# A selective scan laid out as 4 states by 32 channels, with TensorE forming its input term

## The chip, the cores and the metric

The program runs on one NeuronCore of one Trainium2 chip. The metric is the device time of one launch in microseconds; lower is better.

## The reference

The program is two transformer-like layers. The change touches the Mamba block of the second layer. With `x` of 2 sequences by 2048 positions by 256, it computes:

```
xz = layernorm(x) @ w_in            # 512 channels of x_path, 512 of z_path
x_path = silu(conv4(x_path) + b_conv)
B, C = x_path @ w_b, x_path @ w_c   # 16 states each
delta = softplus(x_path @ w_delta + b_delta)
A = -exp(A_log)                     # 512 channels by 16 states
for t:                              # per channel d and state n
    h = exp(delta[t] * A) * h + (delta[t] * x_path[t]) * B[t]
    y[t] = sum over n of h * C[t]  +  D * x_path[t]
out = (y * silu(z_path)) @ w_out
```

Everything is fp32. There are 512 channels, 16 states, and 4096 positions in all (two sequences of 2048, each with its own state).

## The kernel before

The stages run one after the other, each in its own block with an allocator whose prefix names its tiles: attention (`ag`, `qkv`, `att`, `ao`), a mixture of experts (`ex`, `mo`), then `scan_inputs` (tiles `si_...`), `selective_scan` (tiles `ss_...`), and an fp4 feed-forward (`wt`, `fp`). A block ends when all five engines have ended their part of it. Inside a block each engine has its own written-out list of instructions, and semaphores join the lists; nothing reorders them.

**scan_inputs** works on 8 groups of 512 positions (`GROUPS`, `GN`), all 512 channels at once as four tiles of 128 (`DT`). `run_stages` writes one engine's steps for all groups, each step shifted by so many groups. TensorE (PE) forms `xz` from `si_xn_t` (L2014), `delta` before its softplus (L2025), and B and C (L2030). VectorE (DVE) convolves, and makes `xc` (the silu of the convolution, L1903), `zs` and `delta` (L1914). ScalarE (ACT) does the exponentials and logarithms and copies PSUM to SBUF. GpSimd (POOL) multiplies `dx = delta * xc` (L1827). Then `delta` and `dx` are each split into three bf16 parts whose sum is the fp32 value: DVE casts the high part (L1840, L1845), POOL subtracts (L1815, L1817), ACT makes the middle part (L1955). SyncE (SP) stores the six parts, 512 KB each, to `scratch.steps`, and `xc`, `zs`, B and C beside them.

**selective_scan** takes 256 units. A unit is 1024 positions (`HALF`, half a sequence) of 8 channels by 16 states on the 128 partitions; 16 units with the same 128 channels and positions make a part. Per unit: SP loads the six bf16 rows of its 8 channels (`ss_stack`, 96 KB); PE spreads them over the partitions with bf16 tables of ones (`spread_x` into `ss_ps_x`, L2304; `spread_d` into `ss_ps_d`, L2314, which has two slots and so waits for an older scan); ACT makes the decay in place in `ss_ps_d` (L2240); `u` is `ss_ps_x` times B. For two units of three DVE makes `u` (L2254); for the third (`n % 3 == 2`) ACT copies `ss_ps_x` (L2237) and POOL multiplies (L2204). DVE runs the scan (L2266), one instruction over 1024 positions; the second half of a sequence starts from the last column of `h`. POOL multiplies `h` by C (`ss_ch`, L2215). PE sums over states into `ss_ps_y` (`sums`, L2336): four fp32 matmuls of 32 output columns of the array each and 256 positions per unit, five units behind the last of their group of four. Once a part, PE adds D times x (`skip_term`, L2325) and DVE multiplies by `zs` (`gate`, L2274).

## Time and profile before

| | us |
|---|---|
| median of 3 runs | 4137.14 |
| lowest and highest of them | 4123.6, 4149.17 |
| the profiled execution | 4119.56 |
| its span | 4117.7 |
| mean granted TensorE clock in it, as a share of full speed | 0.858 |

All rows below are of the profiled execution. The span is the time from the first to the last instruction; the profiled execution is 1.9 us longer than its span, and 17.6 us shorter than the median. In the span, `scan_inputs` lies at 2388 to 2797, `selective_scan` at 2797 to 3627, the feed-forward behind that. TensorE has two clock levels, 1.2 and 2.4 GHz, which read 0.50 and 1.00 as granted clock.

### The profile page before, as it was taken

What the parts mean: (1) busy time and instruction counts of PE and PEld (TensorE: products, weight loads), DVE (VectorE), ACT (ScalarE), POOL (GpSimd) and SP (SyncE); (2) the same over time, 40 slices, a digit from 0 to 9 for tenths busy, and PEclk for the clock granted to TensorE, in tenths of its full rate; (3) what the DMA queues carried; (4) which work ended last, traced back from release to release, by engine and by line L of the source; (5) the groups of instructions that cost most, each with busy time, mean ns of one, the idle gap of its engine ahead of it and who ended that gap; (6) DMA issues with size and microseconds to landing.
All of it is one profiled execution on the core that took longest, in us unless ns stands there. A gap on an engine that the chain in (4) does not pass through costs nothing. (4 is left out here: it accounts for less than half of the span.)

```text
span 4117.7 us, 50542 instructions
## 1 busy us (share of the span) xinstructions
PE 3344.1 (81%) x16354; PEld 1530.2 (37%) x16355; DVE 3214.5 (78%) x4733; ACT 2031.6 (49%) x2575; POOL 1531.3 (37%) x1012
## 2 busy tenths in 40 slices
PE   5769999999999999695997678646778877847876
PEld 2433333333333333274665433211111111125665
DVE  5659999999999999244442559987999999957996
ACT  0317777777777777531111656643444444415453
POOL 0100000000000000023003605567999999946775
PEclk8869999999999999867999789876776677769998
DMA  1662203031230300332222533332122212121110
GB/s 51 237 158 28 45 4 46 4 45 18 32 45 4 46 4 4 104 123 87 65 65 80 169 107 114 129 124 84 63 70 75 72 63 64 62 72 54 51 41 18
DMA packets 221697, 280.48 MB, mean 68 GB/s; under 512 B 40313, under 2 KB 163458, under 8 KB 218786
## 3 DMA queue, kind: packets, MB, share of 16 engines
q1 hardware_dynamic: 204658, 244.47, 21.8%
q0 software_dynamic: 6144, 17.05, 1.3%
q10 hardware_dynamic: 10688, 16.32, 1.1%
q8 instruction: 116, 1.90, 0.2%
q14 instruction: 91, 0.75, 0.1%
HBM read 152.56 MB, written 124.57 MB: 67 GB/s over the span
## 5 line engine op out<-in xcount | busy, mean ns | idle before, releaser
L909 DVE TENSOR_REDUCE att_maxima<-att_ps_m 128x1 f32<-128x512 f32 x2048 | 1275.4, 682 | 163.4 <-PE att_ps_m L965 158.7
L864 ACT ACTIVATE att_probs<-att_ps_s 128x1024 f32<-128x1024 f32 x1024 | 998.4, 1021 | 383.0 <-PE att_ps_s L980 379.1
L965 PE MATMUL att_ps_m<-att_ks,att_qs 48*128 48x512 f32 x2048 | 743.3, 487 | 71.9 <-DMA att_ks<-scratch_k 28.6
L2215 POOL TENSOR_TENSOR ss_ch<-ss_h,ss_c_rep 128x1024 f32<-128x1024 f32 x256 | 594.1, 2345 | 0.7 <-DVE ss_h L2266 0.6
L965 PEld LDWEIGHTS att_ps_m<-att_ks,att_qs 48*128 48x128 f32 x2048 | 300.0, 188 | 757.7 <-DVE att_maxima L909 650.2
L991 PE MATMUL att_ps_o<-att_probs,att_vs 128*32 128x512 f32 x4096 | 546.4, 605 | 0.5 <-ACT att_probs L864 0.5
L2240 ACT ACTIVATE ss_ps_d<-ss_ps_d,ss_a_neg 128x1024 f32<-128x1024 f32 x256 | 278.6, 1088 | 417.4 <-PE ss_ps_d L2314 417.4
L980 PE MATMUL att_ps_s<-att_qs,att_ks 50*128 50x512 f32 x2048 | 466.1, 401 | 1.8 <-ACT att_probs L864 0.7
L2266 DVE TENSOR_TENSOR_SCAN ss_h<-ss_ps_d,ss_h,ss_u 128x1024 f32<-128x1024 f32 x128 | 296.0, 2334 | 5.5 <-ACT ss_ps_d L2240 2.4
L2314 PE MATMUL ss_ps_d<-ss_stack,ss_spread 96*128 96x512 bf16 x512 | 213.7, 511 | 97.5 <-DVE ss_h L2266 91.9
L2266 DVE TENSOR_TENSOR_SCAN ss_h<-ss_ps_d,ss_u 128x1024 f32<-128x1024 f32 x128 | 288.2, 2274 | 5.9 <-issue 3.1
L980 PEld LDWEIGHTS att_ps_s<-att_qs,att_ks 50*128 50x128 f32 x2048 | 279.2, 186 | 34.1 <-ACT att_probs L864 23.7
L837 POOL TENSOR_TENSOR att_m_parts<-att_m_t,att_m_parts 16x128 fp32r<-16x128 f32 x32 | 14.3, 448 | 737.4 <-ACT att_m_parts L884 737.4
L844 POOL TENSOR_TENSOR att_heads<-att_o_t,att_sums 128x256 f32<-128x256 f32 x32 | 19.9, 621 | 705.2 <-DVE att_sums L924 705.2
L2304 PE MATMUL ss_ps_x<-ss_stack,ss_spread 96*128 96x512 bf16 x512 | 217.7, 519 | 66.8 <-DVE ss_u L2254 61.7
L2336 PE MATMUL ss_ps_y<-ss_ch,ss_sum_block 128*32 128x256 f32 x2048 | 217.8, 511 | 4.0 <-POOL ss_ch L2215 4.0
L2254 DVE TENSOR_TENSOR ss_u<-ss_ps_x,ss_b_rep 128x1024 f32<-128x1024 f32 x171 | 204.7, 1197 | 16.4 <-PE ss_ps_x L2304 16.4
L2204 POOL TENSOR_TENSOR ss_u<-ss_x_copy,ss_b_rep 128x1024 f32<-128x1024 f32 x85 | 199.4, 2345 | 25.7 <-ACT ss_x_copy L2237 25.7
L2014 PE MATMUL si_ps_xz<-si_xn_t,si_w_in 128*128 128x512 f32 x256 | 128.8, 662 | 74.0 <-ACT si_xp L1983 57.4
L1639 POOL DMA_INDIRECT mo_back<-scratch_sorted_y,moe_packed x64 | 61.7, 964 | 339.2 <-DMA mo_b_norm<-in_b_norm 318.4
L1435 ACT ACTIVATE ex_y<-ex_ps_y,ex_x 128x256 f32<-128x256 f32 x72 | 34.2, 475 | 303.1 <-PE ex_ps_y L1506 303.1
L1488 PE MATMUL ex_ps_h<-moe_w_w,ex_x_t 128*128 x288 | 137.4, 600 | 0.4 <-issue 0.4
(404 smaller groups left out, 5026.5 us busy)
## 6 DMA issues: line engine op xcount, KB each, us to landing
...
ss_stack<-scratch_steps SPq DMA_DIRECT2D x256, 96.0 KB
...
```

What stands on the lines that cost most here:

```text
L864: act.activation(probs[:, (2 * n + pair) % 4, :, :], ps_s[pair][:, :, :], ACT.Exp, scale=HD ** -0.5).then_inc(exp_done, 1)
L909: dve.tensor_reduce(maxima[:, j, at:at + 1], ps_m[plan.bank(key)][:, :], AX.X, ALU.max).then_inc(maxed, 1)
L965: pe.matmul(ps_m[plan.bank(key)][:, :], qs[own, s // QC % 2, s % QC, p, t * P:(t + 1) * P], ks[own, s // QC % 2, p, c * GN:(c + 1) * GN], ...
L980: mm = pe.matmul(ps_s[pair][:, e, :], ks[rows_of(e, 0, ROWS), st // QC % 2, pair, kt * P:(kt + 1) * P], qs[rows_of(e, 0, ROWS), st // QC % ...
L991: mm = pe.matmul(ps_o[h * VW:(h + 1) * VW, :], vs[st // QC % 2][:, kt, h * VW:(h + 1) * VW], probs[:, (2 * n + h // 2) % 4, h % 2, :], sta ...
L2215: pool.tensor_tensor(ch[:, w.n % (CH_GROUPS * JQ), :], h[:, w.i, :], c_rep[:, w.half, :], ALU.mult).then_inc(s["ch_ready"], 1)
L2240: act.activation(ps_d[:, w.n % 2, :], ps_d[:, w.n % 2, :], ACT.Exp, scale=a_neg[:, at:at + 1]).then_inc(s["decay_ready"], 1)
L2254: dve.tensor_tensor(u[:, w.n % U_SLOTS, :], ps_x[:, :], b_rep[:, w.half, :], ALU.mult).then_inc(s["u_ready"], 1)
L2266: dve.tensor_tensor_scan(h[:, w.i, :], ps_d[:, w.n % 2, :], u[:, w.n % U_SLOTS, :], start, ALU.mult, ALU.add).then_inc(s["h_ready"], 1)
L2304: mm = pe.matmul(ps_x[:, q * GN:(q + 1) * GN], spread[:, 1, :], stack[:, w.n % STACKS, q * GN:(q + 1) * GN], start=True, stop=True)
L2314: mm = pe.matmul(ps_d[:, w.n % 2, q * GN:(q + 1) * GN], spread[:, 0, :], stack[:, w.n % STACKS, q * GN:(q + 1) * GN], start=True, stop=True)
L2336: mm = pe.matmul(ps_y[jq * 32:(jq + 1) * 32, cols], block[:, jj, :], ch[:, (part * JJ + jj) % CH_GROUPS * JQ + jq, cols], start=False, sto ...
```

## The change

**The scan's layout.** A unit is still 1024 positions and 128 rows of (channel, state), 256 units, 16 to a part, but now 4 states (`NSUB`) by 32 channels (`DSUB`). The order of parts becomes four chunks of 1024 positions, with the four channel tiles inside each; a chunk that is the second of its sequence starts from `ss_carry`, a column that ACT copies out of `h` (`keep_state`). `h` has 4 slots (`H_SLOTS`) where it had 16.

**u.** PE forms `u` by itself (`make_u`): for each 64 positions, `dx` turned (64 positions by 32 channels) is the stationary operand and a diagonal matrix with B of one state on its diagonal (64 by 64, `ss_diag`) the moving one. That is 8 blocks x 2 halves of the array's rows x 4 column groups (the states) = 64 fp32 matmuls a unit, each of 64 rows, 32 output columns and 64 positions, into one of three pairs of PSUM banks (`ss_ps_u`). ACT builds the 512 diagonals in 64 calls of `build_diag`, eight small ACTIVATEs each, from the turned B (`ss_b_t`): 32 ACTIVATEs ahead of the first unit, eight beside each of the next 12 units, and eight beside each of 16 units around every one of the three changes of chunk. The multiplications by B on DVE and POOL, the copies for them and the replicated B are gone.

**The decay.** SP loads fp32 `delta` of 32 channels four times over (`ss_delta`, 512 KB, four per part, six slots), and ACT writes `exp(delta * A)` to SBUF (`ss_decay`, three slots). The scan reads the decay from SBUF and `u` from PSUM, where it read them the other way about. POOL has only `ss_ch` left. The sums and the skip term keep their shapes.

**scan_inputs.** The six bf16 parts, their casts, subtractions and middle copies go. `delta` is stored as fp32 (1 MB a group). DVE makes `dx`; PE turns it (16 transposes of 128 by 128 a group, and 4 small ones for B and C) into the banks that `xz` uses; ACT copies it to SBUF in four copies of 512 columns and one of 128; SP stores it (1 MB). POOL has nothing left but memsets. SP also lays `A_log` out in the scan's order, in 16 transfers of 512 single fp32 elements each.

The diff, cut:

```diff
...
+                with nc.allow_non_contiguous_dma("the scan's order of states and channels"):
+                    by = io["A_log"].rearrange("(l g s) (q h) -> s h (l g) q", l=8, g=4, s=4, h=4)
+                    for state in range(4):
+                        for eight in range(4):
+                            at = (state * 4 + eight) * 8
+                            sp.dma_start(scratch.a_rows[at:at + 8, :].rearrange("l (g q) -> (l g) q", g=4), by[state, eight]).then_inc(s["a_laid"], 16)
...
-                    sp.wait_ge(s["low_ready"], g * 2 + i + 1)
-                    for part in reversed(range(i * PARTS, (i + 1) * PARTS)):
-                        sp.dma_start(tiles(scratch.steps[part, :, :], g), parts[:, part, :, :]).then_inc(s[stored], 16)
...
+                    sp.wait_ge(s["delta_ready"], g + 1)
+                    sp.dma_start(tiles(scratch.delta, g), val[:, slot, 0, :, :]).then_inc(s["delta_stored"], 16)
+                def store_turned(g, slot):
+                    sp.wait_ge(s["dx_copied"], (g + 1) * GT)
+                    sp.dma_start(rows_at(scratch.dx_t, g * GN), dx_t[:, :, :]).then_inc(s["dx_stored"], 16)
+                    sp.wait_ge(s["b_copied"], g + 1)
+                    sp.dma_start(rows_at(scratch.b_t, g * GN), b_t[:, :, :]).then_inc(s["b_stored"], 16)
...
-                def split(i, g, slot):
...
-                    pool.tensor_tensor(v, v, parts[:, i * PARTS, :, :], ALU.subtract).then_inc(s["rest_ready"], 1)
...
-                    pool.tensor_tensor(parts[:, i * PARTS + 2, :, :], v, parts[:, i * PARTS + 1, :, :], ALU.subtract).then_inc(s["low_ready"], 1)
...
-                    pool.wait_ge(s["delta_ready"], g + 1)
-                    pool.tensor_tensor(val[:, slot, 1, :, :], val[:, slot, 0, :, :], xc[:, slot, :, :], ALU.mult).then_inc(s["dx_ready"], 1)
...
-                    dve.tensor_copy(parts[:, 0, :, :], val[:, slot, 0, :, :]).then_inc(s["high_ready"], 1)
...
+                def delta_x(g, slot):
...
+                    dve.tensor_tensor(val[:, slot, 1, :, :], val[:, slot, 0, :, :], xc[:, slot, :, :], ALU.mult).then_inc(s["dx_ready"], 1)
...
-                    act.wait_ge(s["rest_ready"], g * 2 + i + 1)
-                    act.activation(parts[:, i * PARTS + 1, :, :], val[:, slot, i, :, :], ACT.Copy).then_inc(s["mid_ready"], 1)
...
+                def copy_turned(g, slot):
+                    for t in range(GT):
+                        act.wait_ge(s["dx_turned"], g * GT + t + 1)
...
+                        act.activation(dx_t[:, t, :], ps_xz[t % XZ][:, :], ACT.Copy).then_inc(s["dx_copied"], 1)
...
+                    act.activation(b_t[:, :, :].rearrange("p t n -> p (t n)"), ps_xz[GT % XZ][:, 0:GT * 2 * NS], ACT.Copy).then_inc(s["b_copied"], 1)
...
+                def turn(g, slot):
+                    pe.wait_ge(s["dx_ready"], g + 1)
+                    for t in range(GT):
...
+                            pe.wait_ge(s["xz_copied"], (min(g + 3, GROUPS) if isinstance(g, int) else g + 3) * 2 * DT)
...
+                        for o in range(DT):
+                            mm = pe.transpose(ps_xz[t % XZ][:, o * P:(o + 1) * P], val[:, slot, 1, o, t * P:(t + 1) * P], ident[:, :])
+                        mm.then_inc(s["dx_turned"], 1)
+                    for t in range(GT):
+                        mm = pe.transpose(ps_xz[GT % XZ][:, t * 2 * NS:(t + 1) * 2 * NS], bc[:, t * P:(t + 1) * P], ident[0:2 * NS, 0:2 * NS])
+                    mm.then_inc(s["bc_turned"], 1)
...
-                run_stages(pe, GROUPS, (product_xc, 1), (product_xz, -1))
...
+                run_stages(pe, GROUPS, (product_xc, 1), (turn, 2), (product_xz, -1))
...
-STACKS, U_SLOTS = 4, 3
...
+DELTAS, DECAYS, U_BANKS, H_SLOTS = 6, 3, 3, 4
...
-        self.on_pool = n % 3 == 2
-        self.pool = (n + 1) // 3
...
+        self.ng, self.dq = self.i // DQ, self.i % DQ
...
-                    sp.dma_start(stack[0:PARTROWS, w.n % STACKS, :], scratch.steps[:, row:row + DG, w.cols]).then_inc(stack_loaded[w.n % STACKS], 16)
...
+                    sp.dma_start(delta[:, k % DELTAS, :], over(scratch.delta[first:first + DSUB, cols:cols + HALF].unsqueeze(0), [NSUB, DSUB, HALF])
...
+                def load_dx(part):
...
+                    at = part // DT * HALF
+                    for half in range(2):
+                        rows = scratch.dx_t[at + half * (HALF // 2):at + (half + 1) * (HALF // 2), part % DT * P:(part % DT + 1) * P]
+                        sp.dma_start(dx_t[half * RT:(half + 1) * RT, part % 2, :, :], rows.rearrange("(j p) d -> p j d", p=RT)).then_inc(dx_loaded[part % 2], 16)
...
+                    sp.dma_start(c_rep[:, ng, :], over(rows.unsqueeze(1), [NSUB, DSUB, HALF])).then_inc(c_loaded[ng], 16)
...
-                    pool.tensor_tensor(u[:, w.n % U_SLOTS, :], x_copy[:, w.pool % 2, :], b_rep[:, w.half, :], ALU.mult).then_inc(s["pool_u_ready"], 1)
...
+                        pool.wait_ge(s["y_steps"], w.n // DQ - CH_GROUPS + 1)
+                    pool.tensor_tensor(ch[:, w.n % (CH_GROUPS * DQ), :], h[:, w.n % H_SLOTS, :], c_rep[:, w.ng, :], ALU.mult).then_inc(s["ch_ready"], 1)
             @blk.scalar
...
+                for half in range(2):
+                    rows = scratch.b_t[:, 0:NS].rearrange("(c h j p) n -> h p c j n", c=CHUNKS, h=2, p=RT)[half]
+                    for chunk in range(CHUNKS):
+                        act.dma_start(b_t[half * RT:(half + 1) * RT, chunk, :, :], rows[:, chunk, :, :]).then_inc(s["b_loaded"], 16)
...
+                def build_diag(chunk, ng, q):
+                    if chunk > 0 and q == 0:
+                        act.wait_ge(s["u_ready"], (chunk * DT - 1) * GROUPS_HERE + (ng + 1) * DQ)
+                    for m in range(q * PIECE, (q + 1) * PIECE):
+                        j, n = m // NSUB, ng * NSUB + m % NSUB
+                        ins = act.activation(diag[:, j, n, :], ident_two[:, :], ACT.Copy, scale=b_t[:, chunk, j, n:n + 1])
+                    ins.then_inc(s["diag_ready"], 1)
+                def make_decay(w):
...
+                    act.activation(decay[:, w.n % DECAYS, :], delta[:, w.delta % DELTAS, :], ACT.Exp, scale=a_neg[:, at:at + 1]).then_inc(s["decay_ready"], 1)
...
+                    act.activation(carry[:, w.state:w.state + 1], h[:, w.n % H_SLOTS, HALF - 1:HALF], ACT.Copy).then_inc(s["carried"], 1)
...
+                    make_decay(w)
+                    if w.n >= DECAYS and not units[w.n - DECAYS].second:
+                        keep_state(units[w.n - DECAYS])
+                    if w.n < (NG - 1) * DQ:
+                        build_diag(0, w.ng + 1, w.dq)
...
+                    if w.dt == DT - 1 and w.ng > 0 and w.chunk + 1 < CHUNKS:
+                        build_diag(w.chunk + 1, w.ng - 1, w.dq)
+                    if w.dt == 0 and w.ng == 0 and w.chunk > 0:
+                        build_diag(w.chunk, NG - 1, w.dq)
...
-                    dve.tensor_tensor_scan(h[:, w.i, :], ps_d[:, w.n % 2, :], u[:, w.n % U_SLOTS, :], start,
+                    dve.wait_ge(s["u_ready"], w.n + 1)
...
+                    if w.second:
+                        dve.wait_ge(s["carried"], w.carried)
+                        start = carry[:, w.state:w.state + 1]
+                    dve.tensor_tensor_scan(h[:, w.n % H_SLOTS, :], decay[:, w.n % DECAYS, :], ps_u[w.n % U_BANKS][:, :], start,
...
+                    if w.part > 0 and w.i == SUMS_TO - 1:
+                        gate(w.part - 1)
+                    scan(w)
+                gate(PARTS_HERE - 1)
...
+                def make_u(w):
+                    if w.i == 0:
+                        pe.wait_ge(dx_loaded[w.part % 2], (w.part // 2 + 1) * 2 * 16)
+                    if w.dt == 0 and w.dq == 0:
+                        pe.wait_ge(s["diag_ready"], diag_built(w.chunk, w.ng))
+                    if w.n >= U_BANKS:
+                        pe.wait_ge(s["h_ready"], w.n - U_BANKS + 1)
+                    for j in range(BLOCKS):
+                        for half in range(2):
+                            own, at = slice(half * RT, (half + 1) * RT), half * (HALF // 2) + j * RT
+                            for q in range(NSUB):
+                                mm = pe.matmul(ps_u[w.n % U_BANKS][q * DSUB:(q + 1) * DSUB, at:at + RT], dx_t[own, w.part % 2, j, w.dq * DSUB:(w.dq + 1) * DSUB],
+                                               diag[own, j, w.ng * NSUB + q, :], start=True, stop=True)
+                    mm.then_inc(s["u_ready"], 1)
...
-                        mm = pe.matmul(ps_x[:, q * GN:(q + 1) * GN], spread[:, 1, :], stack[:, w.n % STACKS, q * GN:(q + 1) * GN],
...
-                        mm = pe.matmul(ps_d[:, w.n % 2, q * GN:(q + 1) * GN], spread[:, 0, :], stack[:, w.n % STACKS, q * GN:(q + 1) * GN],
...
+                        mm = pe.matmul(ps_y[dq * DSUB:(dq + 1) * DSUB, cols], block[:, :], ch[:, (part * NG + ng) % CH_GROUPS * DQ + dq, cols],
...
                 for w in units:
-                    spread_x(w)
                     if w.i == SUMS_FROM:
-                        skip_term(w)
+                        skip_term(w.part)
                     sums_at(w.n)
-                    spread_d(w)
...
```

PE in the scan, around the skip term of a part, before (`ss_ps_x` and `ss_ps_d` are the spread dx and delta, `ss_ps_y` the output sums):

```order
L2304 MATMUL ss_ps_x<-ss_stack,ss_spread 128x512 x2
L2325 MATMUL ss_ps_y<-ss_xc,ss_skip 128x512 x2
L2336 MATMUL ss_ps_y<-ss_ch,ss_sum_block 32x256 x4
L2314 MATMUL ss_ps_d<-ss_stack,ss_spread 128x512 x2
L2304 MATMUL ss_ps_x<-ss_stack,ss_spread 128x512 x2
L2336 MATMUL ss_ps_y<-ss_ch,ss_sum_block 32x256 x4
```

With the change PE has there (`ss_ps_u` is the input term u, three slots):

```order
L2305 MATMUL ss_ps_u0<-ss_diag,ss_dx_t 32x64 x64
L2317 MATMUL ss_ps_y<-ss_xc,ss_skip 128x512 x2
L2326 MATMUL ss_ps_y<-ss_ch,ss_sum_block 32x256 x4
L2305 MATMUL ss_ps_u1<-ss_diag,ss_dx_t 32x64 x64
L2326 MATMUL ss_ps_y<-ss_ch,ss_sum_block 32x256 x4
L2305 MATMUL ss_ps_u2<-ss_diag,ss_dx_t 32x64 x64
```

The two spreads of two matmuls each become one group of 64; sums and skip term stand ahead of it as they stood ahead of `spread_d`.

ACT at the head of the scan, before:

```order
L2222 ACTIVATE ss_a_neg<-ss_a_neg 128x64
L2224 ACTIVATE ss_skip<-all_ident,ss_d_col 128x128 x4
L2226 ACTIVATE ss_a_neg<-ss_a_neg 128x64
L2229 ACTIVATE ss_b_rep<-ss_ps_d 128x1024
L2231 ACTIVATE ss_c_rep<-ss_ps_d 128x1024
L2240 ACTIVATE ss_ps_d<-ss_ps_d,ss_a_neg 128x1024 x2
L2237 ACTIVATE ss_x_copy<-ss_ps_x 128x1024
```

With the change ACT has there:

```order
L2198 DMA ss_a_neg<-scratch_a_rows 128x64
L2202 DMA ss_b_t<-scratch_b_t 64x8x16 x8
L2203 DMA ss_d_col<-in_D_param 128x4
L2206 ACTIVATE ss_ident_two<-all_ident 64x64 x2
L2209 ACTIVATE ss_sum_block<-all_ident 32x32 x4
L2211 ACTIVATE ss_a_neg<-ss_a_neg 128x64
L2213 ACTIVATE ss_a_neg<-ss_a_neg 128x64
L2221 ACTIVATE ss_diag<-ss_ident_two,ss_b_t 128x64 x32
L2229 ACTIVATE ss_decay<-ss_delta,ss_a_neg 128x1024
L2221 ACTIVATE ss_diag<-ss_ident_two,ss_b_t 128x64 x8
```

The loads of the turned B and 32 diagonals stand ahead of the first decay; the skip tables moved behind the first units.

SP at the head of `scan_inputs`, before:

```order
L1764 DMA si_w_in<-in_w_in 128x2x1024
L1765 DMA si_w_conv<-in_w_conv 128x16
L1767 DMA si_b_conv<-in_b_conv 128x4
L1767 DMA si_b_delta<-in_b_delta 128x4
L1780 DMA si_xn_t<-scratch_xn_t 128x2x512 x3
```

With the change SP has there:

```order
L1765 DMA si_w_in<-in_w_in 128x2x1024
L1766 DMA si_w_conv<-in_w_conv 128x16
L1768 DMA si_b_conv<-in_b_conv 128x4
L1768 DMA si_b_delta<-in_b_delta 128x4
L1775 DMA scratch_a_rows<-in_A_log 512x1x1 x16
L1785 DMA si_xn_t<-scratch_xn_t 128x2x512 x3
```

The 16 transfers of `A_log` stand between the small loads and the first loads of the normalised input.

## Rows read from the trace of the kernel before

**Rows 1.** Windows of the scan: window, length, PE, PEld, DVE, ACT, POOL, PEclk, DMA share, GB/s
```profile
2900.00:3000.00 100.00, 79.67 (x394) 18.64 (x392) 97.69 (x56) 45.07 (x42) 99.21 (x44) 0.72 0.20 63
3001.40:3002.60 1.20, 1.19 (x9) 0.20 (x8) 1.20 (x1) 1.16 (x2) 1.20 (x1) 0.50 0.11 22
3007.00:3007.80 0.80, 0.70 (x9) 0.16 (x8) 0.80 (x1) 0.72 (x1) 0.80 (x2) 1.00 0.00 0
```

**Rows 2.** Groups of the scan, 2820 to 3600: busy us, mean ns, idle
```profile
L2215 POOL TENSOR_TENSOR ss_ch<-ss_h,ss_c_rep 128x1024 f32<-128x1024 f32 x249 | 577.9, 2345 | 0.7 <-DVE ss_h L2266 0.6
...
L2254 DVE TENSOR_TENSOR ss_u<-ss_ps_x,ss_b_rep 128x1024 f32<-128x1024 f32 x166 | 198.7, 1197 | 7.5 <-PE ss_ps_x L2304 7.5
```

**Rows 3.** Lines by source: ns min/median/max, first and last start us
```profile
L2266 DVE TENSOR_TENSOR_SCAN ss_h<-ss_ps_d,ss_u x128: 2251/2276/2292, 2813.4 to 3563.6; 128x1024 f32<-128x1024 f32 x128
L2266 DVE TENSOR_TENSOR_SCAN ss_h<-ss_ps_d,ss_h,ss_u x128: 2311/2336/2351, 2861.6 to 3612.3; 128x1024 f32<-128x1024 f32 x128
...
L2274 DVE TENSOR_TENSOR ss_gated<-ss_ps_y,ss_zs x16: 1189/1216/1225, 2881.9 to 3622.5; 128x1024 f32<-128x1024 f32 x16
```

**Rows 4.** Waits, 2820 to 3600: us in total, times, longest
```profile
ACT ss_ps_d L2240 <- PE ss_ps_d L2314: 407.7, 244, 6.2
...
DVE ss_u L2254 <- PE ss_ps_x L2304: 7.5, 6, 1.7
```

**Rows 5.** Timeline of the scan: start us, us, engine, line, records
```profile
3000.34 4.58 DVE L2266 TENSOR_TENSOR_SCAN ss_h<-ss_ps_d,ss_h,ss_u 128x1024 f32<-128x1024 f32 x2
...
3001.51 1.08 PE L2336 MATMUL ss_ps_y<-ss_ch,ss_sum_block 128*32 128x256 f32 x8
...
3005.30 6.96 POOL L2215 TENSOR_TENSOR ss_ch<-ss_h,ss_c_rep 128x1024 f32<-128x1024 f32 x3
...
3007.06 0.64 PE L2336 MATMUL ss_ps_y<-ss_ch,ss_sum_block 128*32 128x256 f32 x8
...
3610.62 4.13 PE L2336 MATMUL ss_ps_y<-ss_ch,ss_sum_block 128*32 128x256 f32 x40
```

**Rows 6.** Timeline of TensorE in the attention and router stages
```profile
804.42 0.40 PE L980 MATMUL att_ps_s<-att_qs,att_ks 50*128 50x512 f32 x2
...
1857.84 0.24 PE L1368 MATMUL ao_ps_c<-ao_both,ao_all_ones 128*128 128x8 bf16 x4
1857.94 1.07 PE L1335 MATMUL ao_ps_x<-all_ident,moe_rows 128*128 128x128 f32 x8
```

**Rows 7.** Page, part 3: the queue that fetches instructions
```profile
q8 instruction: 116, 1.90, 0.2%
```

**Rows 8.** Line by source: one load of 4096 four-byte pieces
```profile
L815 SPq DMA_DIRECT2D scratch_b_rows<-in_b x1: 14220/14220/14220, 306.8 to 306.8; - x1
```

**Rows 9.** Timeline of the scan's head
```profile
2797.59 0.36 SPq L2109 DMA_DIRECT2D ss_a_neg<-in_A_log  x1
...
2799.86 1.26 ACT L2224 ACTIVATE ss_skip<-all_ident,ss_d_col 128x128 f32<-128x128 f32 x4
...
2805.37 1.02 ACT L2229 ACTIVATE ss_b_rep<-ss_ps_d 128x1024 f32<-128x1024 f32 x1 [4.11 <-PE ss_ps_d L2292]
```

**Rows 10.** Window of scan_inputs, its steady part (columns as in 1)
```profile
2423.20:2721.40 298.20, 228.14 (x492) 92.33 (x492) 284.84 (x198) 182.92 (x179) 144.65 (x30) 0.88 0.34 116
```

**Rows 11.** Line by source: the product that makes xc
```profile
L1903 DVE TENSOR_TENSOR si_xc<-si_conv,si_sig_c x8: 2291/6154/6158, 2423.2 to 2721.4; 128x2048 f32<-128x2048 f32 x8
```

**Rows 12.** Groups of scan_inputs, 2423.2 to 2721.4
```profile
L2014 PE MATMUL si_ps_xz<-si_xn_t,si_w_in 128*128 128x512 f32 x212 | 107.6, 666 | 57.4 <-ACT si_xp L1983 57.4
...
L1840 DVE CAST si_parts<-si_val 128x2048 bf16<-128x2048 f32 x6 | 24.7, 4114 | 0.6
```

**Rows 13.** Timeline of scan_inputs' end
```profile
2720.12 5.32 POOL L1817 TENSOR_TENSOR si_parts<-si_val,si_parts 128x2048 bf16<-128x2048 f32 x1 [2.02 <-ACT si_parts L1955]
...
2764.62 5.53 POOL L1827 TENSOR_TENSOR si_val<-si_val,si_xc 128x2048 f32<-128x2048 f32 x1 [4.56 <-DVE si_val L1914]
...
2786.26 4.05 POOL L1817 TENSOR_TENSOR si_parts<-si_val,si_parts 128x2048 bf16<-128x2048 f32 x1 [2.02 <-ACT si_parts L1955]
```

436 lines of the change are left out of this document (180 added, 256 removed).

## The prediction

> **What bounds the kernel now.** I read the windows first, then the groups and the waits of the scan, then the timeline of single units. In the scan two engines are full at once: in a window of 100 us DVE is busy 97.7 and POOL 99.2, against 80 for PE and 45 for ACT [rows 1]. The waits say the same from the other side: ACT waits 408 us of 780 for PE's spread, while DVE's largest wait on another engine for its own u is 7.5 us [rows 4]. Per unit DVE does a scan of 2.28 or 2.34 us and, for two units of three, a product of 1.20 us; POOL does `ss_ch` at 2.35 us and, for one of three, the same again for u [rows 2, 3]: DVE 2.31 + 0.80 = 3.11, POOL 2.35 x 1.33 = 3.13. The loop runs from the first scan at 2813.4 to the end of the last gate at 3622.5 + 1.2 = 3623.7 [rows 3], 810.3 us or 3.165 a unit. So what DVE and POOL lose, the loop gains, until something else is late. In `scan_inputs` DVE is full too, 284.8 us of 298.2 [rows 10], but not by its own work: the product that makes `xc` takes 2.29 us at best and 6.15 in the median [rows 11], and the last one starts 1.3 us into a subtraction of POOL [rows 11, 13]. Two DVE operations with SBUF operands are stretched by POOL's splits, a cast to 4.1 us among them [rows 12].
>
> **The scan's loop, engine by engine.** DVE keeps scans and gates: two scans in a row take 4.58, so 2.29 each [rows 5]; 256 x 2.29 + 16 x 1.22 = 606 us. POOL keeps `ss_ch`: three in 6.96 [rows 5], 256 x 2.32 = 594. The scan still reads one operand from SBUF and one from PSUM, so I take its price as unchanged. Both engines now end within 2% of each other, and PE and ACT must stay under 2.3 us a unit.
>
> PE: a step of the sums is four fp32 matmuls in four column groups and shows as 8 records, so one such matmul is two passes. The eight take 1.08 us at granted clock 0.50 and 0.64 at 1.00 [rows 1, 5], and a stream of 40 takes 4.13 [rows 5]: ten rounds of four, 0.41 us each at the lower clock for 256 columns. The column groups do run side by side. Two records on the two halves of the array's rows take 0.40 together, as long as one [rows 6], so row halves run side by side as well; both together, eight tiles, no row shows. If they do, `make_u` is 64 x 2 / 8 = 16 rounds of 64 columns: a quarter of 0.41, 0.10 to 0.11 us a round at the lower clock, 1.7 us; at the upper clock a quarter of 0.32 (0.64 / 2), 0.08, so 1.3 us. With the sums (1.08 or 0.64) and 0.2 for the two changes of shape, an estimate, PE needs 3.0 us a unit at the lower clock and 2.1 at the upper. At the mix of before, 0.72 [rows 1], that is 0.56 x 3.0 + 0.44 x 2.1 = 2.6, above the 2.29 of DVE. But PE has three slots of u to run ahead in, and when it is the late one it has no idle time. I take 0.1 us a unit, +26, between 0 and 256 x 0.31 = +79.
>
> ACT: the decay is one pass over 128 x 1024, like the 1.02 us copy [rows 9], and the carried column is small (0.2, an estimate). A diagonal is 128 x 64; four of 128 x 128 took 1.26, 0.315 each [rows 9]. A 64-column one lies between half of that and all of it; I take 0.25. Eight beside a unit are 2.0 us, so ACT needs 3.2 in those units, 0.9 too much. They are 12 + 3 x 16 = 60 units: 54, less what the two decays made ahead cover at each chunk change (3 x 5), 39, and a part of that lies in units where PE is late anyway. I take +30, between 0 (0.16 each) and +90 (0.315 each).
>
> At a part's boundary the gate waits for the last sums, and the skip term, queued ahead of sums and `make_u` on PE, waits for the gate. DVE has two scans, 4.6 us, until it needs that u; skip term, sums and `make_u` need 3 to 4.5. Cost 0 to 20 us over 15 boundaries; I take 10. The loop: 606 + 26 + 30 + 10 = 672, against 810: **-138**.
>
> **The scan's head.** Before, the first scan comes 2813.4 - 2797.6 = 15.8 us after the start [rows 3, 9]. With the change ACT first issues eight loads of 512 pieces of 64 bytes. A transfer of 4096 four-byte pieces occupied its queue for 14.22 us [rows 8], 3.5 ns a piece; I take the same per piece, so 14.2 us for these 4096. Then 2 us of landing, 32 diagonals at 0.25 (8 us) and a first u and decay of 3: 27 to 28. **+12**, between -2 and +18. Nothing hides this: every engine waits for the first u.
>
> **scan_inputs.** Head: the 16 transfers of `A_log` are 8192 four-byte pieces on SP, ahead of the first load of the input, so 8192 x 3.47 ns = 28.4 us in which PE has no input. **+28**, between +6 (if a transfer cost what a small load costs, 0.36 [rows 9]) and +33. Middle: `xc` is made eight times from 2423.2 to 2721.4 [rows 11], 42.6 us apart. Without splits and casts DVE's own work is some 30 us a group, and ACT's about 27. PE is next: 228.1 / 7 = 32.6 [rows 10], 16 + 4 transposes of which eight take 1.07 [rows 6], 2.7, and its waits for ACT's copies, 57.4 / 7 = 8.2 before [rows 12], of which I keep 4.5, as ACT must empty the same banks of the turned dx too. So 39.8 a group, **-18** for seven, between -46 and 0. Tail: delta of the last group is there at 2764.6, the last split ends at 2790.3, and the scan starts 7.3 later [rows 9, 13]. Now delta comes some 6 us sooner (its chain on DVE is no longer stretched), then dx 2.3, turning 2.7, a last copy 0.7, and the same 7.3: 2771.6. **-26**, between -15 and -32. These terms sum to -4 without the scan's loop, with +12 of its head in it.
>
> **Sum.** -138 + 12 + 28 - 18 - 26 = -142 on the profiled execution of 4119.6, so 3978. The median of the runs is 17.6 above that execution; on it the forecast is 4137 - 142 = **3995**.
>
> **The rivals.** First, PE stays at its lower clock. Then it needs 3.0 to 3.1 us a unit and sets the pace: 256 x 3.05 = 781, -29, and with the -4 some **4104**, from 4090 to 4125: no change to speak of. For it: the clock is 0.72 at 80% busy PE [rows 1]. Against: at 3 us a unit PE would be busy all the time, which it is not now.
>
> Second, and on the slower side: **what one matmul costs however short it is**. 64 matmuls of two passes are 128 pairs of weight load and matmul in each unit, with 64 columns each. The densest row of the trace has four bf16 matmuls of 8 columns in 0.24 us, where one takes 0.17 [rows 6]: 23 ns apart, though each has only 8 columns. If such a gap holds between tiles too, `make_u` costs 128 x 23 ns = 2.9 us, with sums and changes 3.8 a unit: 256 x 3.8 + 20 = 993, +183 - 4, **4316**. It decides from 3.1 us a unit on, that is from 17.6 ns a pair. If only the row halves fail to overlap, `make_u` is 32 rounds of 80 to 107 ns, 2.6 to 3.4 us, and the unit 3.4 to 4.7: 4210 and up. The instruction stream works the same way: its queue fetched 116 packets, 1.90 MB [rows 7], one in 35 us, and the change gives PE some 230 more instructions in every unit. Against it: eight records of four tiles fit in 0.64 us, which leaves little room for a gap between tiles, but four tiles of 256 columns would hide one. This is the rule of the Trainium skill that speaks against the change: "TensorE: Matmul & The Clock Gate", section "Wait — 56ns, not 53.3ns?", says that start-to-start never drops below about 25 ns however few the columns. Read as a limit on every pair it would make `make_u` 3.2 us and the time some 4380. The same section gives 62 ns a matmul when decoding is done in software, which would be 7.9 us a unit; the 23 ns of [rows 6] rule that out here.
>
> Third, small ones: diagonals, piece-wise loads and boundaries all at their dear ends, +60 + 6 + 5 + 10 on the forecast, 4076.
>
> **Chances.** The forecast with its own range 3935 to 4080 (PE's cover, ACT's builds, the head's and the input stage's bounds): 0.56. PE at its lower clock: 0.17, of which 0.04 below 4096. The pair cost, row halves or fetch: 0.24, from 4180 to 4400. Something outside these, better or worse: 0.03. The range must reach into the second rival: 3935 to 4290 leaves out about 0.03 below and 0.14 above. One per cent, 41 us, is about what a measurement of this kernel can tell from no change: faster 0.61, same 0.14, slower 0.25.
>
> **What the profile of the changed kernel would show.** Right: scans 2.3 us apart over most of the loop, POOL with next to no idle time, the `make_u` group at 1.3 to 1.7 us from first to last record with eight tiles starting within a few tens of ns, granted clock above 0.75 in the scan, and pauses of DVE only around the chunk changes, ended by ACT's decay. If instead DVE waits mostly for `ss_ps_u`, the granted clock tells the first rival (near 0.5) from the second (near 1.0, pairs 20 ns or more apart). In `scan_inputs` the first `si_xn_t` load should be issued some 28 us later than before, `xc` should come every 40 us at 2.3 us each, and the scan should start about 16 us sooner than before. The prediction fails most likely at the step that lets eight tiles of 64 columns run at the rate of four of 256.

## The result and the profile after

The kernel with the change takes 4412.95 us (median of 4, 4404.66 to 4428.87), against 4141.94 for the kernel before in the same comparison: a ratio of 1.069, 95% interval 1.066 to 1.072. It is slower by 271 us. The forecast was 3995 in a range up to 4290. The profiled execution took 4428.87, its span is 4427.1, 309.4 longer than that of before.

The page, with the head of the span, part 1 (busy us, share, instructions) and the queue that fetches instructions, which answers to [rows 7]:

```profile
span 4427.1 us, 114206 instructions
PE 3409.8 (77%) x48250; PEld 1855.4 (42%) x48251; DVE 2922.0 (66%) x4552; ACT 2080.2 (47%) x3158; POOL 1149.9 (26%) x864
...
q8 instruction: 364, 5.96, 0.6%
```

PE has 48,250 matmul records where it had 16,354, and the instruction queue fetched 364 packets of 16 KB where it had fetched 116. Yet PE's busy time rose by 66 us only, from 3344.1. Windows of 100 us in the scan (columns as in [rows 1], which they answer to):

```profile
3000.00:3100.00 100.00, 67.08 (x3110) 42.75 (x3091) 53.24 (x25) 50.61 (x142) 54.24 (x23) 0.75 0.23 73
3500.00:3600.00 100.00, 62.13 (x3157) 41.33 (x3150) 53.63 (x24) 28.71 (x47) 54.48 (x24) 0.83 0.27 76
```

Nothing is full any more: DVE and POOL fell from 98 and 99 to some 54, PE is at 62 to 67. The granted clock is 0.75 and 0.83 in these two windows, higher than the 0.72 of before. Scans and gates by source (as [rows 3]) and the waits of 2830 to 3900 (as [rows 4]):

```profile
L2273 DVE TENSOR_TENSOR_SCAN ss_h<-ss_decay,ss_ps_u x128: 2260/2287/2290, 2838.0 to 3658.4; 128x1024 f32<-128x1024 f32 x128
L2273 DVE TENSOR_TENSOR_SCAN ss_h<-ss_decay,ss_carry,ss_ps_u x128: 2320/2347/2349, 3106.7 to 3924.8; 128x1024 f32<-128x1024 f32 x128
...
L2281 DVE TENSOR_TENSOR ss_gated<-ss_ps_y,ss_zs x16: 1224/1225/1226, 2929.2 to 3931.7; 128x1024 f32<-128x1024 f32 x16
```

```profile
POOL ss_ch L2194 <- DVE ss_h L2273: 920.3, 235, 444.7
ACT ss_decay L2229 <- DVE ss_h L2273: 594.9, 196, 7.1
...
DVE ss_h L2273 <- PE ss_ps_u L2305: 434.8, 184, 64.8
...
DVE ss_h L2273 <- ACT ss_decay L2229: 27.6, 19, 3.6
```

The durations are those of before. The loop is 3931.7 + 1.2 - 2838.0 = 1094.9 us, 4.28 a unit, where it was 810.3. DVE waits 435 us for `ss_ps_u`, 65 of them before the first scan; the wait for ACT's decay, for which the forecast had a term of 30, is 28. The timeline shows what PE does in that time:

```profile
3300.57 2.35 DVE L2273 TENSOR_TENSOR_SCAN ss_h<-ss_decay,ss_carry,ss_ps_u 128x1024 f32<-128x1024 f32 x1 [1.19 <-PE ss_ps_u L2305]
...
3300.98 0.81 PE L2305 MATMUL ss_ps_u<-ss_diag,ss_dx_t 64*32 64x64 f32 x58
3303.00 2.36 POOL L2194 TENSOR_TENSOR ss_ch<-ss_h,ss_c_rep 128x1024 f32<-128x1024 f32 x1 [1.16 <-DVE ss_h L2273]
...
3303.12 0.93 PE L2305 MATMUL ss_ps_u<-ss_diag,ss_dx_t 64*32 64x64 f32 x70 [1.33 <-issue]
...
3303.97 0.64 PE L2326 MATMUL ss_ps_y<-ss_ch,ss_sum_block 128*32 128x256 f32 x8
...
3304.13 2.35 DVE L2273 TENSOR_TENSOR_SCAN ss_h<-ss_decay,ss_carry,ss_ps_u 128x1024 f32<-128x1024 f32 x1 [1.22 <-PE ss_ps_u L2305]
...
3304.54 0.74 PE L2305 MATMUL ss_ps_u<-ss_diag,ss_dx_t 64*32 64x64 f32 x50
...
3307.26 1.02 PE L2305 MATMUL ss_ps_u<-ss_diag,ss_dx_t 64*32 64x64 f32 x78 [1.98 <-issue]
...
3308.38 2.35 DVE L2273 TENSOR_TENSOR_SCAN ss_h<-ss_decay,ss_carry,ss_ps_u 128x1024 f32<-128x1024 f32 x1 [1.90 <-PE ss_ps_u L2305]
```

In the second row 58 matmul records (an fp32 matmul makes two), each with its weight load, run in 0.81 us, the last of them alone some 0.2: a new pair of load and matmul every 11 ns, so the eight tiles do overlap, as the forecast had it. Then PE does nothing for 1.33 us, in the middle of a `make_u`, and its idle time is put down to "issue": no semaphore is waited for. The next piece has 70 records of `make_u`, 8 of the sums, 50 more, then nothing until 3307.26. From one such stop to the next are 128 pairs of two instructions, 256 instructions, and 256 is what a packet of the instruction queue holds: e1 below has 256 units x 128 = 32,768 PE instructions fewer and 128 packets fewer.

In the trace's records of that queue the loop has 272 packets, as many as 256 units of 272 instructions need, a median of 3.78 us apart and never under 3.25. PE stops for more than 0.8 us 214 times in the loop, 368 us together, with 128 matmul records between two stops in the median. A packet takes 1.1 us; it starts 1.0 us before PE falls silent, and PE starts again 1.4 us after it has ended (medians; eight of ten of these restarts lie between 1.25 and 1.55 us). So what PE waits for is its next packet of instructions.

Where the 309 us went, stage by stage, from the first and last starts of the same operations in both profiles:

| | before | after | difference | forecast |
|---|---|---|---|---|
| up to the start of `scan_inputs` | 2388.2 | 2393.6 | +5.4 | 0 |
| from there to the first xc | 35.0 | 86.9 | +51.9 | +28 |
| seven intervals of xc | 298.2 | 258.2 | -40.0 | -18 |
| last xc to the scan's block | 76.2 | 44.9 | -31.3 | -26 |
| the scan's head | 15.8 | 54.4 | +38.6 | +12 |
| its loop | 810.3 | 1094.9 | +284.6 | -138 |
| the rest | 494.0 | 494.2 | +0.2 | 0 |

The product that makes xc, by source, answers to [rows 11]; it is at its 2.29 us every time, now that POOL is silent. Behind it stands the window of the seven intervals (columns as in [rows 1], answers to [rows 10]):

```profile
L1881 DVE TENSOR_TENSOR si_xc<-si_conv,si_sig_c x8: 2291/2293/2293, 2480.5 to 2738.7; 128x2048 f32<-128x2048 f32 x8
```

```profile
2480.50:2738.70 258.20, 233.08 (x612) 100.77 (x612) 187.92 (x193) 173.41 (x197) 0.00 (x0) 0.98 0.33 119
```

Both heads in the timeline: SP lays out `A_log`, then issues the input's load, and PE's first matmul; ACT's eight loads of the turned B, SP's four of C, the diagonals and the first scan:

```profile
2395.64 37.28 SPq L1775 DMA_DIRECT2D scratch_a_rows<-in_A_log  x16
2433.17 4.88 SPq L1785 DMA_DIRECT2D si_xn_t<-scratch_xn_t  x2
...
2456.49 15.37 PE L2022 MATMUL si_ps_xz<-si_xn_t,si_w_in 128*128 128x512 f32 x32 [68.21 <-DMA si_xn_t<-scratch_xn_t]
...
2783.98 24.87 ACTq L2202 DMA_DIRECT2D ss_b_t<-scratch_b_t  x8
...
2791.53 20.14 SPq L2141 DMA_DIRECT2D ss_c_rep<-scratch_bc  x4
...
2827.95 7.74 ACT L2221 ACTIVATE ss_diag<-ss_ident_two,ss_b_t 128x64 f32<-128x64 f32 x32 [11.91 <-DMA ss_b_t<-scratch_b_t]
...
2837.98 2.29 DVE L2273 TENSOR_TENSOR_SCAN ss_h<-ss_decay,ss_ps_u 128x1024 f32<-128x1024 f32 x1 [64.80 <-PE ss_ps_u L2305]
```

The 16 transfers occupy SP for 37.3 us, 2.3 each, and the load issued behind them lands 23 us later, where it took 7 before. ACT is busy until 2808.9 issuing its eight loads, 24.9 us; the last of them lands 19 us later, at 2827.9, and for the last 12 of these ACT does nothing but wait.

### The profile page after: what moved, and what is told of

Read it like the earlier page. It is cut to its first block and busy times, and to the rows that moved or that the text cites. A ratio compares the mean times of both kernels' runs of the same rounds, so it can differ in the third digit from the quotient of the medians.

```text
span 4427.1 us, 114206 instructions
## 1 busy us (share of the span) xinstructions
PE 3409.8 (77%) x48250; PEld 1855.4 (42%) x48251; DVE 2922.0 (66%) x4552; ACT 2080.2 (47%) x3158; POOL 1149.9 (26%) x864
## 5 line engine op out<-in xcount | busy, mean ns | idle before, releaser
L2194 POOL TENSOR_TENSOR ss_ch<-ss_h,ss_c_rep 128x1024 f32<-128x1024 f32 x256 | 604.5, 2363 | 929.4 <-DVE ss_h L2273 929.3
L2305 PE MATMUL ss_ps_u<-ss_diag,ss_dx_t 64*32 64x64 f32 x32768 | 493.9, 253 | 424.0 <-issue 364.7
L2305 PEld LDWEIGHTS ss_ps_u<-ss_diag,ss_dx_t 64*32 64x32 f32 x32768 | 402.3, 119 | 602.3 <-issue 598.4
L2229 ACT ACTIVATE ss_decay<-ss_delta,ss_a_neg 128x1024 f32<-128x1024 f32 x256 | 293.5, 1147 | 606.5 <-DVE ss_h L2273 605.8
L2273 DVE TENSOR_TENSOR_SCAN ss_h<-ss_decay,ss_ps_u 128x1024 f32<-128x1024 f32 x128 | 292.1, 2285 | 296.8 <-PE ss_ps_u L2305 253.2
L2273 DVE TENSOR_TENSOR_SCAN ss_h<-ss_decay,ss_carry,ss_ps_u 128x1024 f32<-128x1024 f32 x128 | 299.7, 2345 | 211.2 <-PE ss_ps_u L2305 189.5
L2326 PE MATMUL ss_ps_y<-ss_ch,ss_sum_block 128*32 128x256 f32 x2048 | 205.6, 464 | 25.5 <-issue 24.7
L2022 PE MATMUL si_ps_xz<-si_xn_t,si_w_in 128*128 128x512 f32 x256 | 118.2, 617 | 87.7 <-DMA si_xn_t<-scratch_xn_t 68.2
L2221 ACT ACTIVATE ss_diag<-ss_ident_two,ss_b_t 128x64 f32<-128x64 f32 x512 | 128.3, 335 | 69.6 <-PE ss_ps_u L2305 57.7
L1508 PE MATMUL ex_ps_y<-moe_w_w,ex_hid_t 128*128 x576 | 136.1, 379 | 0.0
```

What stands on the lines that cost most here:

```text
L1508: mm = pe.matmul(ps_y[slot][:, 0, :], hid_t[:, slot, f, :], w2[:, bass.ds(e, 1), f, :].rearrange("p a c -> p (a c)"), start=f == 0, stop=f ...
L2194: pool.tensor_tensor(ch[:, w.n % (CH_GROUPS * DQ), :], h[:, w.n % H_SLOTS, :], c_rep[:, w.ng, :], ALU.mult).then_inc(s["ch_ready"], 1)
L2229: act.activation(decay[:, w.n % DECAYS, :], delta[:, w.delta % DELTAS, :], ACT.Exp, scale=a_neg[:, at:at + 1]).then_inc(s["decay_ready"], 1)
L2273: dve.tensor_tensor_scan(h[:, w.n % H_SLOTS, :], decay[:, w.n % DECAYS, :], ps_u[w.n % U_BANKS][:, :], start, ALU.mult, ALU.add).then_inc( ...
L2305: mm = pe.matmul(ps_u[w.n % U_BANKS][q * DSUB:(q + 1) * DSUB, at:at + RT], dx_t[own, w.part % 2, j, w.dq * DSUB:(w.dq + 1) * DSUB], diag[o ...
L2326: mm = pe.matmul(ps_y[dq * DSUB:(dq + 1) * DSUB, cols], block[:, :], ch[:, (part * NG + ng) % CH_GROUPS * DQ + dq, cols], start=False, sto ...
```

## The experiments

The first four ask what holds PE: the array's work (the column theory), or the number of its instructions, which have to be fetched (the fetch theory, later called supply theory).

**e1_wide.** Half the instructions, the same columns.

```diff
-                    for j in range(BLOCKS):
+                    for j in range(0, BLOCKS, 2):
...
-                                mm = pe.matmul(ps_u[...][..., at:at + RT], dx_t[...], diag[own, j, w.ng * NSUB + q, :], ...)
+                                two = w.ng * NSUB + q // 2 * 2
+                                mm = pe.matmul(ps_u[...][..., at:at + 2 * RT], dx_t[...], diag[own, j, two:two + 2, :], ...)
```

> The kernel with the change, but make_u issues 32 matmuls of 128 columns a unit where it issued 64 of 64: the same columns, half the instructions. The moving operand is two neighbouring diagonals, so half of u is formed with the wrong one. Fetch theory (PE's instructions arrive in blocks of 16 KB, 364 for the whole program, and PE stands still for 1.5 to 2 us at each new one): PE instructions in a unit fall from 272 to 144, blocks in the scan from about 250 to about 135, the loop from 1095 us to 650 to 780, the time to 3970 to 4110, and the instruction queue shows some 120 packets fewer. Column theory (the array is slow on eight tiles): the columns are the same, so the time stays within 1% of 4413.

Measured: 3990.90 us, ratio 0.966 (0.964 to 0.969); loop 651.7. The page's row of the instruction queue, and a window of the scan:

```profile
q8 instruction: 236, 3.87, 0.4%
```

```profile
3200.00:3300.00 100.00, 82.08 (x2986) 47.37 (x2969) 93.79 (x45) 59.84 (x123) 97.32 (x42) 0.98 0.38 118
```

128 packets fewer, and DVE and POOL are full again, at 94 and 97. The same columns on the array fit in the time. The column theory falls.

**e2_short.** Half the columns, the same instructions. DVE also zeroes the banks of u once, before the first unit.

```diff
-                                mm = pe.matmul(ps_u[...][..., at:at + RT], dx_t[...], diag[own, j, w.ng * NSUB + q, :], ...)
+                                mm = pe.matmul(ps_u[...][..., at:at + RT // 2], dx_t[...], diag[own, j, w.ng * NSUB + q, 0:RT // 2], ...)
```

> The kernel with the change, but the 64 matmuls of make_u have 32 columns where they had 64: half the columns, the same instructions. Half of u is left at zero. Fetch theory: blocks and their stops stay, the time stays within 1% of 4413. Column theory: make_u takes half, some 0.6 us less a unit or more, the time 4413 - 150 = 4260 or lower.

Measured: 4436.31 us, ratio 1.073 (1.070 to 1.075), 0.5% above the change; loop 1104.6. Halving the columns gained nothing, with the same 364 packets:

```profile
q8 instruction: 364, 5.96, 0.6%
```

```profile
3300.00:3400.00 100.00, 65.21 (x3047) 39.78 (x3043) 54.82 (x24) 56.32 (x154) 54.26 (x24) 0.53 0.27 76
```

The granted clock is 0.53 here, where the change had 0.75 and 0.83, and the loop is the same to 1%. By itself this leaves a doubt, since half the columns at a lower clock can be as much time on the array; the trace removes it. Packets are 3.78 us apart in both. Where 128 records lie between two stops, the run takes 2.62 us here and the stop behind it 1.23, in the change 2.16 and 1.60 (medians): a longer run has a shorter stop, and run and stop are 3.75 us together in both. PE starts again 1.4 us after a packet's end in both, too. The pace is the packets', not the array's.

**e3_bf16.** Half the instructions and a quarter of the array's time.

```diff
-        diag = r.sb("diag", [P, BLOCKS, NS, RT])
-        dx_t = r.sb("dx_t", [P, 2, BLOCKS, P])
+        diag = r.sb("diag", [P, BLOCKS, NS, RT], BF16)
+        dx_t = r.sb("dx_t", [P, 2, BLOCKS, P], BF16)
```

> The kernel with the change, with the turned dx and the diagonals in bf16, which leaves out the lower part of both: one pass a matmul where fp32 takes two, so half the instructions and a quarter of the array's time in make_u. Fetch theory: 144 PE instructions a unit and nothing else on PE: loop 610 to 720, time 3930 to 4050. If DVE and POOL then set the pace, scans come 2.3 us apart over long stretches, as the forecast had it. If something outside PE (ACT's diagonals, loads) is what holds the scan, the time stays above 4250.

Measured: 3988.24 us, ratio 0.964 (0.962 to 0.967); loop 651.6. Its timeline:

```profile
3201.20 15.35 DVE L2273 TENSOR_TENSOR_SCAN ss_h<-ss_decay,ss_ps_u 128x1024 f32<-128x1024 f32 x7 [1.05 <-PE ss_ps_u L2305]
...
3203.57 13.95 POOL L2194 TENSOR_TENSOR ss_ch<-ss_h,ss_c_rep 128x1024 f32<-128x1024 f32 x6 [0.91 <-DVE ss_h L2273]
...
3205.74 0.57 PEld L2305 LDWEIGHTS ss_ps_u<-ss_diag,ss_dx_t 64*32 64x32 bf16 x64 [0.41 <-DVE ss_h L2273]
...
3206.35 0.16 PEld L2326 LDWEIGHTS ss_ps_y<-ss_ch,ss_sum_block 128*32 128x32 f32 x8
...
3208.96 0.49 PE L2305 MATMUL ss_ps_u<-ss_diag,ss_dx_t 64*32 64x64 bf16 x42 [1.77 <-issue]
```

Seven scans in 15.35 us, six products of POOL in 13.95: 2.2 and 2.3 us apart, as the forecast wanted them. PE still stops (the last row, 1.77 us of "issue"), but it has run ahead by then and nobody waits. Over the whole loop DVE's larger wait is for ACT's decay: 94.3 us ahead of all scans, 63.0 of them before the first one, so 31 inside the loop (34 in e1). The row of the scans that start from zero, the first one's 63.0 among its 86.1:

```profile
L2273 DVE TENSOR_TENSOR_SCAN ss_h<-ss_decay,ss_ps_u 128x1024 f32<-128x1024 f32 x128 | 283.4, 2270 | 94.4 <-ACT ss_decay L2229 86.1 <-issue 4.3 <-PE ss_ps_u L2305 4.0
```

**e9_bf16_96.** A dose between: e3 with 96 matmuls a unit.

```diff
-                    for j in range(BLOCKS):
+                    for j in (*range(BLOCKS // 2), *range(BLOCKS)):
```

> The bf16 version with the first four of its eight blocks formed twice: 96 matmuls a unit where it had 64, 208 PE instructions a unit where it had 144 and the change has 272, and on the array still less work than the change. Supply theory (PE gets no more than one block of 256 instructions in about 3.8 us, 14.8 ns an instruction): 208 x 14.8 ns = 3.1 us a unit, loop some 800 to 860, the time 4130 to 4200. Rival (a version in bf16 is fast because its array work is small): 0.3 to 0.5 us more array work in a unit that has room for it, the time stays within 1% of 3988.

Measured: 4161.31 us, ratio 1.011 (1.008 to 1.013); loop 835.3. Its packets and the stop in its timeline:

```profile
q8 instruction: 300, 4.92, 0.5%
```

```profile
3301.00 0.54 PEld L2305 LDWEIGHTS ss_ps_u<-ss_diag,ss_dx_t 64*32 64x32 bf16 x55 [0.41 <-issue]
...
3303.55 0.56 PE L2305 MATMUL ss_ps_u<-ss_diag,ss_dx_t 64*32 64x64 bf16 x42 [1.89 <-issue]
```

The array has less to do than in the change, and the kernel is 1.1% slower than the one before. The loop has 208 packets, 3.81 us apart (median), as in the change, though pairs start only 7 ns apart here. The supply theory named 800 to 860 for this loop from 14.8 ns an instruction, and it came out at 835. The three doses, with PE instructions a unit: 144 (e1, e3) 652 us, 208 (e9) 835, 272 (change, e2) 1095 and 1105.

**e5_more104 and e4_more52.** Instructions added to the kernel before.

```diff
+                    for m in range(104):        # e4: 52
+                        own = slice(m % 4 * 32, (m % 4 + 1) * 32)
+                        pe.matmul(ps_x[own, m * 8:(m + 1) * 8], spread[:, 1, own], stack[:, w.n % STACKS, m * 8:(m + 1) * 8], start=True, stop=True)
                     for q in range(HALF // GN):
                         mm = pe.matmul(ps_x[:, q * GN:(q + 1) * GN], spread[:, 1, :], ...)
```

> The kernel before, with 104 more matmuls of 8 columns on rotating column groups ahead of each spread_x, which write the values that spread_x then writes again: 208 more PE instructions a unit, hardly any columns. Fetch theory: some 0.85 of a block more per unit, each with a stop of 1.5 to 2 us; before has 0.15 us of slack a unit on DVE and some 0.6 on PE, so the loop grows from 810 by 150 to 400 us and the instruction queue shows some 210 packets more. Rival (eight tiles of fp32 are slow in themselves, instructions are free but for their issue): 104 pairs at 7 to 11 ns are 0.7 to 1.1 us a unit, mostly in PE's idle time, so the time grows by less than 130 us and there are no stops of over 1 us.

Measured: 4408.68 us, ratio 1.066 (1.064 to 1.068), with 208 packets more. The number lies where the fetch theory put it, but the trace gives another cause. PE's timeline and a window:

```profile
3299.82 1.03 PE L2307 MATMUL ss_ps_x<-ss_stack,ss_spread 96*128 96x512 bf16 x2
3300.79 1.08 PE L2339 MATMUL ss_ps_y<-ss_ch,ss_sum_block 128*32 128x256 f32 x8
3301.80 1.03 PE L2317 MATMUL ss_ps_d<-ss_stack,ss_spread 96*128 96x512 bf16 x2
3302.77 0.99 PE L2305 MATMUL ss_ps_x<-ss_stack,ss_spread 96*32 96x8 bf16 x104
```

```profile
3300.00:3400.00 100.00, 94.18 (x2686) 34.56 (x2684) 72.29 (x41) 33.23 (x31) 70.95 (x32) 0.55 0.24 77
```

PE is busy 94% at a granted clock of 0.55 and hardly stops: 1.0 + 1.1 + 1.0 + 1.0 us a unit, in the order of the rows, are its own work at the lower clock, 4.1 of the 4.25 us that a unit takes. The 232 instructions of a unit would come in 3.4 us at 14.8 ns each, so the supply is seldom what ends last: stops of over 0.8 us are 35, 66 us together, against 214 and 368 us in the change (those that there are end 1.5 us after a packet, as elsewhere). So e5 is no test of the supply; most of its cost is PE's own time at the lower clock. The half dose asks whether this reading holds.

> The kernel before, with 52 more matmuls of 8 columns a unit ahead of spread_x, half of the earlier dose of 104. That dose cost 276 us, with PE 94 to 96% busy at a granted clock of 0.53 and few stops: PE's own time at the lower clock, not the supply. By that reading 52 cost PE 0.5 us a unit, 4.2 - 0.5 = 3.7 us a unit at the lower clock, +100 to +150 us. By the supply theory alone 128 instructions a unit are 1.9 us and cost nothing, within 1% of before.

Measured: 4217.63 us, ratio 1.024 (1.020 to 1.028), +100 us, with PE 93 and 96% busy at a clock of 0.62 and 0.59 (the same windows as e5's, 3000 to 3100 and 3300 to 3400). That fits PE's own time, at the low end of its forecast, and not "nothing". How much of e4 and e5 is the added instructions and how much the clock, 0.72 before, was not separated.

**e8_bf16_arows and e7_bf16_heads.** The two heads, on top of e3.

```diff
 # e8: in scan_inputs
-                            sp.dma_start(scratch.a_rows[at:at + 8, :]..., by[state, eight]).then_inc(s["a_laid"], 16)
+                            pool.dma_start(scratch.a_rows[at:at + 8, :]..., by[state, eight]).then_inc(s["a_laid"], 16)
 # e7: and in selective_scan
-                    for chunk in range(CHUNKS):
-                        act.dma_start(b_t[..., chunk, :, :], rows[:, chunk, :, :]).then_inc(s["b_loaded"], 16)
+                    act.dma_start(b_t[..., 0, :, :], rows[:, 0, :, :]).then_inc(s["b_loaded"], 16)
...
-                for k in range(DQ):
-                    load_delta(k)
-                for ng in range(NG):
+                load_delta(0)
+                load_c(0, 0)
+                for k in range(1, DQ):
+                    load_delta(k)
+                for ng in range(1, NG):
                     load_c(0, ng)
...
```

> The bf16 version with the 16 transfers of A_log issued by POOL instead of SP. If they cost what the trace of the change shows (the first load of the input is issued 37 us later and lands 23 us after that, against 7 before), the first xc comes 40 to 50 us sooner and the time is 3940 to 3950. If POOL's queue still delays the input's load through the shared DMA engines, only the 37 us or less come back, and if POOL's issue runs into the end of the stage, nothing does.

Measured: 3958.54 us, ratio 0.962 (0.959 to 0.965), above the 3940 to 3950 that were expected. Against e3's ratio of 0.964 that is some 8 us, within both intervals. From the stage's start to the first xc it is 69.9 us, against 89.6 in e3: 20 us came back in the trace, half of what was expected. The timeline shows where the rest stayed:

```profile
2381.80 10.36 POOL L1818 DMA_DIRECT2D scratch_a_rows<-in_A_log  x16
2382.03 59.48 SPq L1779 DMA_DIRECT2D si_xn_t<-scratch_xn_t  x3
...
2425.03 16.08 PE L2023 MATMUL si_ps_xz<-si_xn_t,si_w_in 128*128 128x512 f32 x32 [50.55 <-DMA si_xn_t<-scratch_xn_t]
```

POOL is done with the 16 in 10.4 us and SP issues the input's load at once, but PE gets it 43 us later. So the 8192 pieces of four bytes cost more than the time to issue them: they hold the load back in the DMA engines too, although it comes from another queue. e10 below tries this by moving them out of the load's way.

> As the last one, and at the scan's head ACT loads the turned B of the first chunk only, SP the other three behind its first loads, and SP loads the first delta and the first C ahead of the other deltas. The change's scan starts 54 us after its block, behind a queue of 6 MB and eight loads that ACT issues at 3 us each. Expected: first scan 20 to 30 us after the block's start, the time 25 to 35 us below the last version, some 3915, the lowest of all. If the landing of what is needed first is not what the first scan waits for, it stays at 3945.

Measured: 3933.36 us, ratio 0.956 (0.953 to 0.958), 25 us below e8 on the same chip; the scan starts 21.2 us after its block (e3 53.9, e8 53.1). Both are inside what was expected; the total of 3915 was missed, since e8 itself had come out higher than forecast; of the 32 us that the head gained, the loop gave 9 back (661 against 652).

**e10_bf16_late and e11_fp32_heads.** One more wait ahead of POOL's transfers, with all cures on the bf16 version and on the change itself.

```diff
+                pool.wait_ge(s["xz_ready"], 3 * 2 * DT)
                 with nc.allow_non_contiguous_dma("the scan's order of states and channels"):
```

> The bf16 version with both cures of the heads, and POOL issues the 16 transfers of A_log only after PE has formed three groups of xz. Issued at the start, POOL spent 10 us on them, but the input's first load still landed 43 us after its issue, so the DMA engines were full of four-byte pieces. If that is the cause, the first xc comes 35 us after the stage's start, as before the change, against 70, and the time is 30 to 40 us below e7, 3895 to 3905. If the pieces now delay later loads and stores of the stage by as much, the time stays at 3933.

Measured: 3913.69 us, ratio 0.946 (0.942 to 0.949), the lowest of all, 9 us above the range that was expected; the first xc comes after 35.6 us, as before the change, where e7 had 70. Against e7's ratio that is 1% or 40 us, against its median in another comparison 20. The traces can't decide between the two: e10's `scan_inputs` starts 21 us later than e7's, behind stages that are the same in both.

> The kernel with the change in fp32 as it is, with the same three cures of the heads. They are worth about 52 us in the input stage and 33 at the scan's head in the trace; if they and the instruction supply of PE are separate terms, the time is 4413 - 85 = 4330 and stays slower than before by 4.5 to 5%. If the supply is eased by the quieter DMA engines too, it falls below 4250.

Measured: 4334.41 us, ratio 1.048 (1.045 to 1.052). 85 us were expected from the heads; 79 came by the medians, 85 by the ratios (1.069 to 1.048). The loop is 1080.0, 15 us or 1.4% less than in the change, and its packets are 3.75 us apart. So the heads and the supply are separate terms, but for those 15 us at most.

## Why the prediction was wrong

**What bounds the kernel before, what DVE, POOL and ACT would cost: right.** Scans, gates and `ss_ch` kept their durations. With PE's instructions halved (e1, e3) the loop is 652 us where the forecast had 672. ACT's diagonals were given 30 us of DVE's waiting; all its waits for the decay inside the loop are 28 in the change, 31 in e3 and 34 in e1, and eight diagonals take 2.0 us beside a unit, as worked out. That the times of e1 and e3, 3991 and 3988, are so near the forecast of 3995 is in part luck: a loop 20 us shorter than forecast stands against other stages that cost 23 us more in the change than their sum said.

**The step that failed** is the price of `make_u`, "at the lower clock, 1.7 us; at the upper clock 1.3 us", and with it "PE needs 3.0 us a unit at the lower clock and 2.1 at the upper". The array's share of this held: pairs start 11 ns apart, 1.4 us for the 128 of a unit, and eight tiles overlap. What was left out of the sum is that PE's 272 instructions a unit have to arrive. They came at 3.8 us for each 256, 14.8 ns an instruction, so 4.0 us a unit; it was 4.28, since some packets are further apart: the 46 gaps over 4.3 us add 74 us to the loop beyond 3.78 each. e2 (same instructions, half the columns, same time), e1 (half the instructions, same columns, 443 us less of loop) and e9 (the dose between) show that it is the instructions and not the array, and the stops, each of which ends 1.4 us after a packet, show that it is their arrival.

**The rival that came true, for another reason.** The second rival gave 4316 at 3.8 us a unit and 17.6 ns a pair as the point from which it decides. The outcome is of that kind: 272 instructions at 14.8 ns are 31 ns for each of the 128 pairs. But its mechanism, a gap of 23 ns between pairs on the array, is refuted by the rows: pairs are 11 ns apart while they last. The fetch was named in it, with its count of packets and "some 230 more instructions" a unit (it is 272 - 24 = 248), and given no price. Its chance of 0.24 was too low, since the one quantity in the change without any row near it, one packet a unit where before had one in 35 us, was bounded from neither side, and the range ended at 4290. The sign that was to tell the two rivals apart, a clock near 0.5 or near 1.0 with pairs 20 ns apart, told neither: the clock was 0.75 and 0.83 and pairs were 11 ns apart.

The floor of 25 ns from start to start that the Trainium skill states ("TensorE: Matmul & The Clock Gate", "Wait — 56ns, not 53.3ns?") does not hold between tiles of this case, which start 11 ns apart. Of the supply, "Runtime: NRT & Kernel Launch", section "Instruction fetch mechanics", says that instructions come in blocks of 16 KiB, 256 instructions, which agrees with the packets here, and that crossing to a new block is mostly hidden. Here it was hidden in the kernel before, mostly hidden in e5 too, and in the change it was not: 3.8 us a block.

**PE at its lower clock**, the first rival, did not happen in the change: the granted clock was 0.75 and 0.83 in the windows shown, 0.72 before. e2 had 0.53, and its time was within 0.5% of the change's.

**The heads** were mis-sized. The 8192 four-byte pieces were taken at 3.47 ns each, from a transfer of another shape; SP took 4.6 (37.3 us), and the load behind them landed 16 us later after its issue than before, for which the sum had no term. The scan's head was +12 in the sum and measured +38.6: each of ACT's loads took 3.1 us to issue where 1.8 was assumed, and the last landed 19 us behind its issue where 2 was assumed, while SP had some 6 MB of loads under way. **The input stage's middle** gained 40 where 18 was taken, inside the bounds: xc comes every 36.9 us, not every 39.8. PE is busy 33.3 us of them where the sum had 32.6 + 2.7, and the granted clock there is 0.98 where [rows 10] have 0.88, which the sum left as it was; PE's other time is 3.6 where 4.5 was kept. The tail gained 31 against 26. The forecast's sum of these four was -4; it measured +19.
